# Perceiver attention kernel: where the second scores pause, and which step two projections stand in

## The chip, the cores and the metric

One core of a Trainium2 chip runs the whole program. The metric is the device time of one execution in microseconds (us); lower is better. The engines of the core run side by side and meet at semaphores: PE (TensorE, matmuls; PEld is its loading of weights), ACT (ScalarE, activations and evictions from the accumulator memory PSUM), DVE (VectorE, reductions and elementwise work), POOL (GpSimd, elementwise work) and SP, which issues the DMAs.

## The reference

There are 16 batches of 64 queries, a context of 1601 rows of width 256, and 16 heads of width 16. What matters here is the first part, cross attention whose temperature depends on statistics of its own scores:

```
K = ctx @ Wk.T + bk ; V = ctx @ Wv.T + bv ; Q = layernorm(x) @ Wq.T + bq
qk = Q . K                                  # per head, 64 x 1601
scores = qk / sqrt(16)
feats = [mean(scores), mean(max(scores)), mean(var(softmax(scores)))]
hidden = gelu(w1 feats + b1); hidden = gelu(w2 hidden + b2)
t = exp(clip(w3 hidden + b3, ln 0.1, ln 10))
out = softmax(qk / (2 t)) @ V ; x = x + out @ Wo.T + bo
```

After it come a gated recurrent layer and a feed-forward layer with quantised weights ("the tail"); they are computed for two batches at a time.

## The kernel before, in words

**Slots and steps.** The order of the work is written out by hand. A batch has a slot, and a slot has 32 steps; every engine walks through the same steps and takes from each its own part. In slot b the kernel computes the first scores of batch b, the statistics and the temperature of batch b-1, and the second scores (with the temperature) and the values of batch b-1 from step 14 on; those reach into steps 0 to 11 of the next slot. A tail piece of earlier batches lies in between. Below, a *full slot* is one in which all of this is there: slots 1 to 15 have first scores, statistics and projections (slot 1 has no second scores in its steps 0 to 11). Slot 0 has no statistics, slot 16 no first scores and no projections.

**First scores.** Unit u (step u) is one pair of heads, which takes 32 of the 128 rows of PE, against 400 keys (`scores`, L651); it shows as two matmul rows. DVE takes its maximum (`maxima`, L1179), ACT its exponential one step later (`exp1`, L909), DVE the sums of that two steps later (`sums`, L1185). There are three PSUM banks, so unit u on PE waits until ACT has done the exponential of unit u-3. PE issues units two at a time, in even steps. `S1_P` says which head pair a step takes, and so which row group (pair modulo 4).

**Second scores and values.** Unit v is one row group of one context tile of 256 rows (13 half tiles, 7 tiles, 4 row groups: 28 units). `S2_AT` is the list of the steps that units 0 to 27 stand in, with the steps of `S2_IDLE` left out: with (36, 37), which are steps 4 and 5 of the next slot, units 18 to 21 stand in steps 0 to 3, 22 and 23 in steps 6 and 7, 24 to 27 in steps 8 to 11. The row group of a unit is that of the first scores' pair two further, so that a first and a second score of one step take different row groups of PE. `scores2` (L667 adds a row, L677 the products) waits for the exponential of the unit two before, `exp2` (L918, ACT) comes one step later, `values` (L694) two steps after the scores and only where a unit stood two steps before; it waits for that unit's `exp2`.

**Projections.** `PJ_PLAN` gives the step in which PE projects the keys ("k", L605 or L612 by the form) or the values ("v") of a context tile: ("k", 4, 0) is the keys of tile 4 of the slot's own batch, a last number of 1 is the next batch's. In the profile the keys' matmuls are L605 (pjp<-cr,wkv) and the values' L612 (pjp<-wkv,cr), 12 to a projection. All projections use the one bank pjp: each waits (`pj_free`) until ACT has evicted the one before (L869 and L882), and ACT does that in the step after, behind `exp2` and `exp1` of that step. A projection of tile 5 must come behind the second scores (keys) or the values (values) that still read tile 5 of the batch before in the same buffer.

**Temperature.** `statistics` on DVE in steps 1, 3, 8 and 10. `temperature` on PE in steps 5, 6 and 7 (L631, L634, L636): in odd steps behind the step's projection, in step 6 between the second scores and the values. Between them ACT runs `gelu` (L888), at the end of step 5 and at the head of step 6, ahead of `exp2`, `exp1` and the eviction of step 6. Gelu and exp need different tables on ACT: there is an ACT_TABLE_LOAD ahead of the first gelu and one ahead of the next exponential.

**The context.** ACT splits a tile into a rounded part (`split_context`, L900), POOL makes the remainder one step later (L1083). Tile 5 is split in step 1, tile 6 in step 9. SP loads the raw tile for the next batch as soon as POOL is done with it.

Of the kernel before, what the change touches and what calls it, by code (L numbers as in the profile page):

```python
# [22 lines left out]
NPAIR = H // 2  # L23
# [35 lines left out]
def unit1(u):  # L59

    return u // NPAIR, S1_P[u]

# [1 line left out]

PJ_PLAN = [(1, ("k", 4, 0)), (5, ("v", 4, 0)), (7, ("k", 5, 0)), (9, ("v", 5, 0)), (11, ("k", 6, 0)),
           (12, ("v", 6, 0)), (13, ("m",)), (17, ("k", 0, 1)), (19, ("v", 0, 1)), (21, ("k", 1, 1)), (23, ("v", 1, 1)),
           (25, ("k", 2, 1)), (27, ("v", 2, 1)), (29, ("k", 3, 1)), (31, ("v", 3, 1))]
N_M = sum(w[0] == "m" for _, w in PJ_PLAN)  # L70
N_OLD = sum(w[0] != "m" and w[-1] == 0 for _, w in PJ_PLAN)
N_NEW = len(PJ_PLAN) - N_M - N_OLD

CTX_AT = {1: (5, 0), 9: (6, 0), 11: (0, 1), 15: (1, 1), 20: (2, 1), 24: (3, 1), 28: (4, 1)}
UNTIL = [(lo + w - 1) // (2 * P) for lo, w in CH]
S2_IDLE = (36, 37)
S2_AT = [s for s in range(14, 14 + S2U + 2) if s not in S2_IDLE]
S1_P = [0, 1, 2, 3, 6, 7, 4, 5, 2, 3, 0, 1, 4, 5, 6, 7] + 2 * list(range(NPAIR))
STATS_AT = [1, 3, 8, 10]
MLP_AT = {5: 0, 6: 1, 7: 2}  # L80
N_MLP = len(MLP_AT)
# [52 lines left out]
class Slot:  # L134
# [91 lines left out]
    def plan(self):  # L226

        got = []
        for step, what in PJ_PLAN:
            if what[0] == "m":  # L230
# [28 lines left out]
def build(nc, t, q_dram, out):  # L259
    ctx = ExitStack()  # L260
    with ctx:
# [298 lines left out]
        def _(pe):  # L560
# [93 lines left out]
            def unit2(v):  # L654

                k = 2 * (v // PPB)
                return k, (S1_P[S2_AT[v] % STEPS] + 2) % PPB, [min(P, SK - P * (k + i)) for i in range(min(2, KTILES - k))]

# [827 lines left out]
```

## Time and profile before

| what | us |
|---|---|
| median of 3 runs | 1311.03 (1310.67 to 1316.09) |
| the profiled execution's own time | 1311.66 |
| its span | 1309.4 |
| PE busy | 1155.3 (88%) |
| PE loading weights | 928.9 (71%) |
| DVE busy | 822.0 (63%) |
| ACT busy | 768.2 (59%) |
| POOL busy | 403.0 (31%) |

The span is the time between the first and the last event of the trace; the execution's own time is 2.3 us more. PE leads by far; no other engine is busy for two thirds of the span. The share of the DMA engines is small (10% of 16 engines). The mean granted clock of PE was 0.861 of full speed; it has two levels, 2.4 and 1.2 GHz (1.00 and 0.50 in the rows).

### The profile page before, as it was taken

The page shows a single profiled execution, that of the slowest core. Times are in us where ns is not written, and L with a number is a line of the kernel's source. Part 1 is how long each engine was busy: PE and PEld are TensorE (multiplying, and loading weights), DVE is VectorE, ACT ScalarE, POOL GpSimd, SP SyncE. Part 2 cuts the span into 40 slices and gives each one's busy share as a digit, 9 for nine tenths or more (in the row PEclk, how much of TensorE's full clock was granted, in tenths as well). Part 3 has the DMA queues.
Part 4 walks back from the last instruction along what each step waited for, and adds up shares of the span by engine and source line. Part 5 has one row for each costly group of instructions (what it writes and reads, how often), then busy time and mean ns, then how long its engine had stood idle before and what let it go on. Part 6 is the DMA issues. An engine that isn't in the chain of part 4 may idle for free.

```text
span 1309.4 us, 39200 instructions
## 1 busy us (share of the span) xinstructions
PE 1155.3 (88%) x14964; PEld 928.9 (71%) x14964; DVE 822.0 (63%) x2124; ACT 768.2 (59%) x1547; POOL 403.0 (31%) x416
## 2 busy tenths in 40 slices
PE   3767898989899989999899989998999989998935
PEld 3545687868787877878687878787777878776622
DVE  3458665656666766767666766676776766772232
ACT  2434486757666765667566766676566756672300
POOL 2366441313234313333233323431333323301210
PEclk9868697969888987989798988899898979995865
DMA  4500110101010101010110101010101000000000
GB/s 122 187 19 25 29 26 14 54 22 35 14 38 10 50 11 42 19 34 26 26 35 14 46 7 45 11 50 10 42 19 35 26 17 3 3 11 2 2 5 4
DMA packets 46812, 38.85 MB, mean 30 GB/s; under 512 B 14576, under 2 KB 46000, under 8 KB 46640
## 3 DMA queue, kind: packets, MB, share of 16 engines
q1 hardware_dynamic: 46640, 36.41, 10.2%
q8 instruction: 125, 2.05, 0.6%
q14 instruction: 47, 0.39, 0.1%
HBM read 34.30 MB, written 2.10 MB: 28 GB/s over the span
## 4 chain that ended last, share of the span: by engine, by line
PE 65%; DVE 16%; issue 9%; ACT 5%; POOL 2%; DMA 1%; SPq 1%; DVEq 0%; ACTq 0%; POOLq 0%
PE pjp L605 11%; PE pjp L612 11%; PE s2p L677 10%; PE s1p L651 10%; PE pvp L694 7%; DVE est L1185 4%; DVE negm L1179 3%; PE tlp L808 2%; PE tlp L790 2%; PE tlp L784 2%; PE s2p L667 1%; PE tlp L751 1%; PE tlp L771 1%; DVE feat L1202 1%; ACT ering L909 1%
## 5 line engine op out<-in xcount | busy, mean ns | idle before, releaser
L1179 DVE TENSOR_REDUCE negm<-s1p 128x1 f32<-128x400 f32 (+1 forms) x512 | 289.3, 565 | 227.1 <-PE s1p L651 222.5
L909 ACT ACTIVATE ering<-s1p,negm 128x400 f32<-128x400 f32 (+1 forms) x512 | 305.6, 597 | 142.7 <-DVE negm L1179 138.0
L918 ACT ACTIVATE pring<-s2p 128x512 f32<-128x512 f32 (+1 forms) x448 | 251.9, 567 | 152.4 <-PE s2p L677 151.9
L651 PE MATMUL s1p<-kt,qbd 32*128 32x400 f32 (+1 forms) x1024 | 301.0, 597 | 15.8 <-ACT ering L909 13.7
L1185 DVE BATCH_NORM_STATS2 est<-ering 128x6 f32<-128x400 f32 (+1 forms) x512 | 290.3, 567 | 23.4 <-ACT ering L909 23.4
L605 PE MATMUL pjp<-cr,wkv 128*128 128x256 f32 (+1 forms) x1344 | 219.4, 321 | 70.6 <-ACT vt L869 45.7
L605 PEld LDWEIGHTS pjp<-cr,wkv 128*128 128x128 f32 x1344 | 196.1, 223 | 87.8 <-issue 58.5
L677 PE MATMUL s2p<-q2bd,kt 32*128 32x128 f32 (+1 forms) x3328 | 249.7, 284 | 0.0
L677 PEld LDWEIGHTS s2p<-q2bd,kt 32*128 32x128 f32 (+1 forms) x3328 | 240.6, 195 | 7.5
L1083 POOL TENSOR_TENSOR cr<-stage,cr 128x512 fp32r<-128x512 f32 (+1 forms) x112 | 132.0, 1179 | 268.7 <-ACT cr L900 268.7
L612 PE MATMUL pjp<-wkv,cr 128*128 128x256 f32 (+1 forms) x1200 | 191.8, 314 | 11.7 <-ACT kt L882 11.4
L612 PEld LDWEIGHTS pjp<-wkv,cr 128*128 128x128 f32 (+1 forms) x1200 | 167.3, 208 | 30.2 <-ACT kt L882 17.7
L651 PEld LDWEIGHTS s1p<-kt,qbd 32*128 32x128 f32 x1024 | 99.1, 202 | 78.9 <-ACT ering L909 38.3
L1069 POOL TENSOR_TENSOR ksum<-ksum,kt 128x512 f32<-128x512 f32 (+1 forms) x80 | 82.6, 1033 | 225.8 <-ACT kt L882 225.7
L694 PE MATMUL pvp<-pring,vt 128*32 128x64 f32 x6656 | 151.2, 234 | 0.2
L694 PEld LDWEIGHTS pvp<-pring,vt 128*32 128x32 f32 x6656 | 112.3, 117 | 53.2 <-issue 24.4
L667 PE MATMUL s2p<-shrow,ones_r 32*128 32x512 f32 (+1 forms) x448 | 127.3, 503 | 5.9 <-ACT pring L918 4.6
L882 ACT ACTIVATE kt<-pjp 128x512 f32<-128x512 f32 (+1 forms) x112 | 61.7, 551 | 53.5 <-PE pjp L605 51.5
L1178 DVE COPY feat<-s1p 128x2 f32<-128x2 f32 x128 | 19.7, 154 | 87.8 <-PE s1p L651 87.2
L869 ACT ACTIVATE vt<-pjp 128x512 f32<-128x512 f32 (+1 forms) x108 | 61.0, 565 | 19.0 <-PE pjp L612 14.3
L900 ACT ACTIVATE cr<-stage 128x512 fp32r<-128x512 f32 (+1 forms) x112 | 65.3, 583 | 10.2 <-DMA stage<-in_ctx 10.2
L667 PEld LDWEIGHTS s2p<-shrow,ones_r 32*128 32x128 f32 (+1 forms) x448 | 48.0, 184 | 24.9 <-ACT pring L918 15.8
(186 smaller groups left out, 1008.8 us busy)
## 6 DMA issues: line engine op xcount, KB each, us to landing
stage<-in_ctx SPq DMA_DIRECT2D x96, 256.0 KB, 2.9
qbd<-q_dram SPq DMA_DIRECT2D x128, 8.0 KB, 1.7
stage<-in_ctx SPq DMA_DIRECT2D x16, 65.0 KB, 2.6
vt<-in_x SPq DMA_DIRECT2D x1, 1024.0 KB, 7.1
q_dram<-late SPq DMA_DIRECT2D x1, 1024.0 KB, 4.7
late<-in_x SPq DMA_DIRECT2D x8, 128.0 KB, 2.1
out_y<-late SPq DMA_DIRECT2D x8, 128.0 KB, 1.7
late<-in_gate SPq DMA_DIRECT2D x1, 768.0 KB, 5.0
```

The costliest lines, as they stand in the source:

```text
L605: mm = nc.tensor.matmul(bank[:, 2 * P * g:2 * P * g + n], wkv[:, 0, wp, d, P * g:P * g + P], c[:, cp, d, 0:n], start=(cp + wp + d == 0), s ...
L612: mm = nc.tensor.matmul(bank[0:m, D * j:D * j + D], c[:, cp, d, P * j:P * j + m], wkv[:, 1, wp, d, :], start=(cp + wp + d == 0), stop=((cp ...
L651: nc.tensor.matmul(s1p[u % 3][:, 0:w], qbd[s.par][rows, g, :], kt[s.par][rows, g, lo:lo + w], start=True, stop=True).then_inc(s1_full, 1)
L667: nc.tensor.matmul(s2p[v % 2][0:ms[0], 0:DB * P * n], ones_r[rows, 0:ms[0]], shrow[rows, :, :].unsqueeze(1).to_broadcast([RT, n, DB, P]), ...
L677: mm = nc.tensor.matmul(s2p[v % 2][0:ms[i], at:at + P], kt[1 - s.par][rows, g, lo:lo + ms[i]], q2bd[1 - s.par][rows, g, :], start=False, s ...
L694: mm = nc.tensor.matmul(pvp[32 * q:32 * q + 32, SQ * r:SQ * r + SQ], vhead(1 - s.par, k + i, ms[i], g, r, j), pring[0:ms[i], v % NPR, at:a ...
L909: nc.scalar.activation(ering[:, u % 3, 0:w], s1p[u % 3][:, 0:w], ACT.Exp, bias=negm[s.par][:, p, c:c + 1]).then_inc(s1_exp, 1)
L918: nc.scalar.activation(pring[0:m, v % NPR, 0:n], s2p[v % 2][0:m, 0:n], ACT.Exp).then_inc(s2_exp, 1)
L1069: nc.gpsimd.tensor_tensor(ksum[:, :, 0:m], was, k[:, :, 2 * P * w:2 * P * w + m], ALU.add).then_inc(ks_part, 1)
L1083: nc.gpsimd.tensor_tensor(c[:, 1, :, 0:n], stage[:, w, :, 0:n], c[:, 0, :, 0:n].bitcast(F32), ALU.subtract).then_inc(ctx_lo, 1)
L1179: nc.vector.tensor_reduce(negm[s.par][:, p, ch:ch + 1], s1p[u % 3][:, 0:w], AX.X, ALU.max, negate=True).then_inc(s1_max, 1)
L1185: nc.vector.bn_stats(est[:, p, ch, :], ering[:, u % 3, 0:CH[ch][1]]).then_inc(s1_sum, 1)
```

## The change

Three constants. The two steps without second scores become 38 and 39 (steps 6 and 7 of the next slot) in place of 36 and 37 (steps 4 and 5), so units 22 and 23 stand in steps 4 and 5. Their values follow two steps later, so `values` has nothing in step 8 in place of step 6. The values' projection of tile 4 goes from step 5 to step 3, the keys' projection of tile 5 from step 7 to step 5; step 7 has none. The order of the head pairs in steps 4 to 7 becomes 4, 5, 6, 7 in place of 6, 7, 4, 5, which keeps the four row groups of tile 5 complete.

```diff
-PJ_PLAN = [(1, ("k", 4, 0)), (5, ("v", 4, 0)), (7, ("k", 5, 0)), (9, ("v", 5, 0)), (11, ("k", 6, 0)),
+PJ_PLAN = [(1, ("k", 4, 0)), (3, ("v", 4, 0)), (5, ("k", 5, 0)), (9, ("v", 5, 0)), (11, ("k", 6, 0)),
            (12, ("v", 6, 0)), (13, ("m",)), (17, ("k", 0, 1)), (19, ("v", 0, 1)), (21, ("k", 1, 1)), (23, ("v", 1, 1)),
...
-S2_IDLE = (36, 37)
+S2_IDLE = (38, 39)
 S2_AT = [s for s in range(14, 14 + S2U + 2) if s not in S2_IDLE]
-S1_P = [0, 1, 2, 3, 6, 7, 4, 5, 2, 3, 0, 1, 4, 5, 6, 7] + 2 * list(range(NPAIR))
+S1_P = [0, 1, 2, 3, 4, 5, 6, 7, 2, 3, 0, 1, 4, 5, 6, 7] + 2 * list(range(NPAIR))
```

## Rows read from the trace of the kernel before

**Rows 1.** The waits from 100 us on: engine, line, releaser: us in total, times, longest.
```profile
PE pjp L605 <- ACT vt L869: 42.0, 15, 2.8
```
**Rows 2.** Timeline of PE, one slot, steps 2 to 12: start, us, then idle before.
```profile
616.89 0.60 PE L651 MATMUL s1p<-kt,qbd 32*128 32x400 f32 x2
...
618.23 0.65 PE L694 MATMUL pvp<-pring,vt 128*32 128x64 f32 x32
618.81 0.94 PE L651 MATMUL s1p<-kt,qbd 32*128 32x400 f32 x2
620.25 0.94 PE L651 MATMUL s1p<-kt,qbd 32*128 32x400 f32 x2 [0.50 <-ACT ering L909]
...
621.69 1.68 PE L612 MATMUL pjp<-wkv,cr 128*128 128x256 f32 x12
623.31 0.52 PE L631 MATMUL tlp<-fm,w1m 128*64 128x16 f32 x6
...
625.73 0.39 PE L634 MATMUL tlp<-hid,w2s 64*128 64x16 f32 x2 [0.18 <-ACT hid L888]
628.95 2.93 PE L605 MATMUL pjp<-cr,wkv 128*128 128x256 f32 x12 [2.83 <-ACT vt L869]
631.80 0.61 PE L636 MATMUL tlp<-hid,w3b 64*128 64x16 f32 x2
632.34 1.03 PE L651 MATMUL s1p<-kt,qbd 32*128 32x400 f32 x2
...
633.97 1.08 PE L694 MATMUL pvp<-pring,vt 128*32 128x64 f32 x32
634.98 2.80 PE L612 MATMUL pjp<-wkv,cr 128*128 128x256 f32 x12
637.71 0.60 PE L651 MATMUL s1p<-kt,qbd 32*128 32x400 f32 x2
...
641.04 0.94 PE L651 MATMUL s1p<-kt,qbd 32*128 32x400 f32 x4
```
**Rows 3.** Timeline of ACT in the same slot, steps 2 and 5 to 7.
```profile
616.71 0.60 ACT L882 ACTIVATE kt<-pjp 128x512 f32<-128x512 f32 x1
...
624.11 1.28 ACT L888 ACT_TABLE_LOAD   x1
...
626.44 1.28 ACT L909 ACT_TABLE_LOAD   x1
627.74 0.59 ACT L909 ACTIVATE ering<-s1p,negm 128x400 f32<-128x400 f32 x1
628.23 0.59 ACT L869 ACTIVATE vt<-pjp 128x512 f32<-128x512 f32 x1
```
**Rows 4.** The same slot on DVE and POOL: the statistics' last part; tile 5's remainder.
```profile
615.82 1.27 POOL L1083 TENSOR_TENSOR cr<-stage,cr 128x512 fp32r<-128x512 f32 x1 [6.31 <-ACT cr L900]
...
622.42 0.37 DVE L1225 TENSOR_SCALAR fm<-r,cst 128x8 f32<-128x8 f32 x2
```
**Rows 5.** Timeline of PE in the slot after it.
```profile
691.55 1.79 PE L651 MATMUL s1p<-kt,qbd 32*128 32x400 f32 x4
...
697.61 0.39 PE L634 MATMUL tlp<-hid,w2s 64*128 64x16 f32 x2 [0.19 <-ACT hid L888]
...
706.86 2.70 PE L612 MATMUL pjp<-wkv,cr 128*128 128x256 f32 x12
```
**Rows 6.** Windows: length, busy us of PE, PEld, DVE, ACT, POOL, then PE's clock, DMA.
```profile
605.60:609.00 3.40, 2.38 (x31) 2.15 (x32) 1.91 (x6) 1.89 (x5) 0.67 (x1) 1.00 0.28 77
...
647.70:651.10 3.40, 2.83 (x34) 1.67 (x36) 3.21 (x10) 2.61 (x6) 0.00 (x0) 1.00 0.44 119
651.10:654.60 3.50, 3.50 (x44) 3.15 (x36) 3.28 (x9) 1.18 (x3) 2.18 (x4) 0.51 0.00 0
...
627.30:637.50 10.20, 8.55 (x72) 7.44 (x72) 2.92 (x7) 6.00 (x14) 1.64 (x2) 0.50 0.01 2
...
132.40:152.90 20.50, 17.56 (x66) 13.31 (x68) 10.91 (x27) 8.09 (x19) 6.44 (x5) 0.50 0.08 20
```
**Rows 7.** Timeline of PE in slot 0: the values' projection of tile 5.
```profile
63.79 2.73 PE L612 MATMUL pjp<-wkv,cr 128*128 128x256 f32 x12 [3.66 <-ACT kt L882]
```

## The prediction

> **What bounds the kernel now.** I read the page's busy times first: PE is busy for 88% of the span and nothing else for two thirds, so what counts is where PE waits or runs slowly. The waits come next: from 100 us on, 15 keys' projections wait for ACT's eviction of the values' tile, 42.0 us together, 2.8 each [rows 1]. That is one wait in each of the full slots 1 to 15. The timeline of one slot shows its shape [rows 2]. PE finishes the second small matmul of the temperature at 625.73 + 0.39 = 626.12 and starts the keys' projection of tile 5 (step 7) at 628.95, after 2.83 idle. What it waits for is bank pjp, still holding the values of tile 4 (step 5, done at 623.31). ACT could evict them in step 6 only behind both gelus: a table load at 624.11, gelu, gelu, a load back at 626.44, one exponential at 627.74, the eviction at 628.23 to 628.82 [rows 3]. So ACT is closed to PE for 3.6 us (624.11 to 627.74), and the old order puts the one bank that PE needs behind it.
>
> The windows then show a second cost. PE's granted clock is 0.50 for the 10.2 us from 627.30 on [rows 6]. In it a values' projection takes 637.71 - 634.98 = 2.73 from start to start, against 623.31 - 621.69 = 1.62 at the high clock [rows 2]: 0.41 of dense time at the low clock is loss.
>
> Third, in step 4, where only two first scores stand, they follow each other: 618.81 and 620.25, with 0.50 idle for an exponential [rows 2]; in the next slot they take 1.79 [rows 5]. A pair that does not wait takes 0.94 (641.04, step 12) [rows 2]: the second unit waits there for `exp1` of unit 2, which is late behind the statistics on DVE.
>
> **The change part by part.** No instruction is added or removed; each has the work of before. So I lay PE's work out again from the end of step 2's values to the end of step 9's projection. Prices from start to start [rows 2]: a group of two first and two second scores 618.23 - 616.89 = 1.34; values 0.58; a projection 1.62; the temperature's first matmuls 0.52; a lone pair 0.94. At the low clock: the temperature's third 632.34 - 631.80 = 0.54, a group 1.63 (632.34 to 633.97).
>
> *Old:* from 618.81 to the start of step 9's projection at 634.98 is 16.17.
>
> *New, step 3:* the values of tile 4, 618.81 to 620.43. Its bank is free: ACT evicted tile 4's keys at 616.71 to 617.31 [rows 3]. This covers the late exponential of unit 2.
> *Step 4:* a whole group, to 621.77, and the values of units 20 and 21, to 622.35.
> *Step 5:* the keys of tile 5, to 623.97. Tile 4's values are evicted in ACT's step 4, in which it had idled; tile 5's remainder was made by POOL at 615.82 to 617.09 [rows 4]. Then the temperature's first, to 624.49; its inputs are ready at 622.79 [rows 4].
> *Step 6:* a lone pair, to 625.43. The table load at 624.11 stood in front of the gelu whether or not PE had come, and I take it to start there again, so the temperature's second is at 625.73 as before, to 626.12. ACT goes through gelu and load to 627.74, then `exp2` of unit 23, 0.59, to 628.33. PE has only the values of unit 22 (0.3) meanwhile, and waits to 628.45 for those of unit 23: some 2.0 us idle, which the change does not remove. It now stands in front of 0.5 us of values and no longer of a projection.
> *Steps 7 and 8:* at the low clock, values 0.5, the temperature's third 0.54, then a group of 1.63 in which first score 9 needs the exponential of unit 6. That comes behind `exp1` of unit 5 and the eviction of tile 5's keys. At ACT's spacing of 0.49 (627.74 to 628.23) [rows 3] it ends near 629.8, so I add 0.2. No values in step 8. Step 9's projection starts near 631.3, 3.7 earlier than 634.98.
>
> The next slot is like it, but PE there starts step 4 at 691.55, and 1.62 + 1.34 + 0.58 + 1.62 + 0.52 + 0.94 = 6.62 puts the temperature's second at 698.17, 0.56 later than the 697.61 of before. With the same 5.57 from there (631.3 - 625.73) the projection starts at 703.74, 3.1 before the old 706.86 [rows 5].
>
> **What the clock takes back.** If PE's low stretch begins and ends where it did, step 9's projection ends 3.7 earlier but 637.5 - 634.0 = 3.5 us of later work now falls into the low stretch, and loses 0.41 x 3.5 = 1.4. Net 3.7 - 1.4 = 2.3 in the one slot, 3.1 - 1.3 = 1.8 in the other, 2.05 as the mean, x 15 = 31. In other words: with the clock as it was, the gain is idle time and the lone pair, and not the slow projection.
>
> **Slots 0 and 16.** In slot 0 one projection more stands ahead of first scores 6 and 7, behind which DVE and POOL have their step's part of the weights' quantisation: at worst 2.7 later (the duration of a projection there); against it the wait of 3.66 for the eviction of the keys of tile 5, which now come two steps earlier, may go [rows 7]. I take 1 lost, between -3.7 and +2.7. Slot 16 I cost at nothing: it has no projections, and its second scores 22 and 23 still wait for the same exponentials.
>
> **Queues passed.** No DMA is moved. On SP tile 5's raw load waits for POOL in step 2, tile 6's in step 10, neither moved. POOL's key sum of tile 5 comes two steps earlier, in an idle stretch. ACT's evictions leave steps 6 and 8 for 4 and 6; the one in step 6 is again behind the gelus, but no projection waits for it until step 9. If that cover went, the old 2.8 would be back. What follows on PE from step 10 on waits only for work that comes earlier by the same amount.
>
> Sum: 1311.66 - 31 + 1 = 1281.7 for the profiled execution; it stood 0.6 above the median, so about 1281 as a median.
>
> **Rivals.**
> *A, the low clock gets shorter.* The idle piece is shorter (2.0 for 2.83) and less of what follows is slow. For it: a stretch of 3.4 with PE busy for 2.38 kept the full clock. Against it: another with 2.83 of 3.40 busy was followed by a low one [rows 6]. With 3.5 us less of low clock the 1.4 is not lost: 15 x 1.4 = 21 more, 1260. If it is gone altogether, the old losses go too (projections 2.93 - 1.68 and 2.80 - 1.68, values 1.08 - 0.65, a group 0.3: 3.1 a slot, x 15 = 47): 1281 - 47 = 1234.
> The Trainium skill, "TensorE: Matmul & The Clock Gate", section "HAM oscillation — how this bites in real kernels", says that a loop whose waits are long enough drops the clock in every iteration, and one with more work between them stays warm. By that rule alone the shortened wait might bring the 1234; the trace bears the first half out (low in each of these slots), and its drop after 2.83 of 3.40 busy speaks against the second.
> *B, the gain is smaller.* The wait at the gelus stays 2.8 instead of 2.0 (the first scores of step 8 also wait for ACT), and step 4's group is held by an exponential. About 1.1 less a slot: 31 - 16 = 15, so 1297.
> *C, the wait only moves.* If PE's chain is set by ACT through all of steps 5 to 9, PE gets nothing: 1311. Against it: the eviction and both exponentials behind the load are 0.49 apart, and PE's first wait is over at 628.45.
> *D, slower.* The low stretch gets longer, because what follows the wait is now thin (small matmuls, a pair that waits) where it was a dense projection. Slot 1, which has no second scores there, was low for 20.5 us [rows 6]. At 0.41 lost, ten more microseconds cost 4.2 a slot against 2.05 won: 15 x 2.15 = 32 slower, 1343. It decides from 5.0 us longer on (15.2 in place of 10.2). Against it: the step 9 projection and the group behind it are as dense as before.
> *E, the change isn't what it says* (the reordering kept PE in another order than the steps): not seen here, PE's rows follow the steps.
>
> **How the numbers follow.** Forecast 0.52 (1271 to 1291 by itself), A 0.24 (1234 to 1271), B 0.12, C 0.05, D 0.06, others 0.01. The time is that of the forecast. The range, 1243 to 1298, holds the forecast, B and all of A but its far end. About 0.5% is what a measurement can tell from no change; below 1304.5 are the forecast, A and B, 0.88; within it C and a part of B and D, 0.06; above it 0.06.
>
> **What would show it.** No wait of 2.8 for the values' eviction ahead of a keys' projection; the 42.0 of [rows 1] under 5. In its place 15 waits near 2.0 ahead of a values group, released by ACT's `exp2` (L918), right behind the second table load. Step 4 with a whole group and no 0.50; step 6 with a pair of 0.94. The keys of tile 5 at 1.6 to 1.7 instead of 2.9. The low stretch near 10 us a slot (A: near 7; D: 15 or more). A temperature's first matmul that comes earlier, or a wait above 2.8 there, would make it wrong.

## The result and the profile after

The changed kernel takes 1264.23 us as the median of 4 runs (1259.24 to 1266.11), against 1311.09 for the kernel before (4 runs, 1310.67 to 1316.09). The ratio is 0.9628, 95% interval 0.9591 to 0.9665: 47 us or 3.7% faster. The time lies in the stated range, but not where the forecast had put it (1281, own range 1271 to 1291); it lies where rival A stood (1260).

First the page of the changed kernel: busy time, share of the span, instructions.

```profile
span 1261.0 us, 39200 instructions
PE 1128.2 (89%) x14964; PEld 910.9 (72%) x14964; DVE 822.1 (65%) x2124; ACT 769.0 (61%) x1547; POOL 402.9 (32%) x416
```

The same 14964 matmuls take PE 27.1 us less busy time (1155.3 before), and the other engines as much as before. The span fell by 48.4, so 27.1 is shorter busy time and 21.3 is less idle time. Not all of the 27.1 is the clock, since busy time also holds what a pair waits inside. By the two levels and the mean granted clocks of the two executions (0.861 and 0.874), the time at the low level fell from 364 to 318 us; with the 0.41 of the prediction that is an estimate of 19 of the 27.1. The waits of PE for ACT in the changed kernel, over its whole run (us in total, times, longest):

```profile
PE pvp L694 <- ACT pring L918: 28.6, 15, 1.9
PE s1p L651 <- ACT ering L909: 10.1, 11, 2.5
...
PE pjp L605 <- ACT vt L869: 2.4, 3, 1.6
```

The 42.0 us of [rows 1] are gone from the keys' projection. In their place stand 15 waits of 1.9 ahead of values, released by the exponential (L918). One slot on PE, which answers to [rows 2]:

```profile
596.27 0.66 PE L694 MATMUL pvp<-pring,vt 128*32 128x64 f32 x32
596.85 1.68 PE L612 MATMUL pjp<-wkv,cr 128*128 128x256 f32 x12
598.46 0.60 PE L651 MATMUL s1p<-kt,qbd 32*128 32x400 f32 x2
...
600.67 1.68 PE L605 MATMUL pjp<-cr,wkv 128*128 128x256 f32 x12
602.28 0.52 PE L631 MATMUL tlp<-fm,w1m 128*64 128x16 f32 x6
602.74 0.94 PE L651 MATMUL s1p<-kt,qbd 32*128 32x400 f32 x4
603.77 0.39 PE L634 MATMUL tlp<-hid,w2s 64*128 64x16 f32 x2
604.09 0.43 PE L694 MATMUL pvp<-pring,vt 128*32 128x64 f32 x16
606.43 0.65 PE L694 MATMUL pvp<-pring,vt 128*32 128x64 f32 x16 [1.91 <-ACT pring L918]
607.01 0.61 PE L636 MATMUL tlp<-hid,w3b 64*128 64x16 f32 x2
...
609.51 2.80 PE L612 MATMUL pjp<-wkv,cr 128*128 128x256 f32 x12
612.24 0.60 PE L651 MATMUL s1p<-kt,qbd 32*128 32x400 f32 x2
```

From the end of step 2's values (596.85) to step 9's projection (609.51) it is 12.66, where it was 16.17. Both projections ahead of the wait now take 1.68, and the keys of tile 5 no longer 2.93; step 9's still takes 2.80, at the low clock. The lone pair takes 0.94. On ACT, the same moment, which answers to [rows 3]: the values' eviction now stands ahead of the loads, and behind them the exponential that PE waits for.

```profile
599.09 0.60 ACT L869 ACTIVATE vt<-pjp 128x512 f32<-128x512 f32 x1
...
602.15 1.28 ACT L888 ACT_TABLE_LOAD   x1
...
604.48 1.28 ACT L918 ACT_TABLE_LOAD   x1
605.78 0.60 ACT L918 ACTIVATE pring<-s2p 128x512 f32<-128x512 f32 x1
```

The low stretch of this slot and of the next, in windows (columns as in [rows 6]):

```profile
598.40:605.00 6.60, 6.03 (x96) 4.75 (x94) 5.63 (x18) 4.82 (x9) 0.00 (x0) 1.00 0.00 0
605.00:611.80 6.80, 5.37 (x42) 4.48 (x43) 3.16 (x8) 4.39 (x10) 1.18 (x1) 0.52 0.01 2
...
676.70:680.10 3.40, 3.40 (x22) 2.74 (x22) 2.37 (x6) 2.20 (x7) 1.24 (x2) 0.53 0.00 0
```

It is 6.8 us long in the one and 3.4 in the other, where it was 10.2 in both slots that the prediction used. The second of those, in the kernel before:

```profile
699.00:709.20 10.20, 8.37 (x71) 7.26 (x72) 3.14 (x8) 6.04 (x14) 4.34 (x4) 0.50 0.01 2
```

### The profile page after: what moved, and what is told of

Same layout as the page of the kernel before. It is cut to its first block, busy times and chain, and to the rows that moved or that the text cites. A ratio compares the mean times of both kernels' runs of the same rounds, so it can differ in the third digit from the quotient of the medians.

```text
span 1261.0 us, 39200 instructions
## 1 busy us (share of the span) xinstructions
PE 1128.2 (89%) x14964; PEld 910.9 (72%) x14964; DVE 822.1 (65%) x2124; ACT 769.0 (61%) x1547; POOL 402.9 (32%) x416
## 3 DMA queue, kind: packets, MB, share of 16 engines
q8 instruction: 125, 2.05, 0.7%
## 4 chain that ended last, share of the span: by engine, by line
PE 70%; DVE 12%; issue 8%; ACT 5%; POOL 2%; DMA 1%; SPq 1%; ACTq 0%; DVEq 0%; POOLq 0%
PE s1p L651 12%; PE s2p L677 12%; PE pjp L612 12%; PE pjp L605 11%; PE pvp L694 8%; DVE est L1185 2%; PE tlp L808 2%; DVE negm L1179 2%; PE tlp L790 2%; PE tlp L784 2%; PE s2p L667 2%; PE tlp L771 1%; ACT pring L918 1%; PE tlp L751 1%; PE tlp L729 1%
## 5 line engine op out<-in xcount | busy, mean ns | idle before, releaser
L918 ACT ACTIVATE pring<-s2p 128x512 f32<-128x512 f32 (+1 forms) x448 | 251.4, 565 | 158.5 <-PE s2p L677 158.0
L651 PE MATMUL s1p<-kt,qbd 32*128 32x400 f32 (+1 forms) x1024 | 292.3, 594 | 12.5 <-ACT ering L909 10.1
L605 PE MATMUL pjp<-cr,wkv 128*128 128x256 f32 (+1 forms) x1344 | 203.7, 306 | 26.5 <-DVE vt L1151 18.4
L605 PEld LDWEIGHTS pjp<-cr,wkv 128*128 128x128 f32 x1344 | 181.6, 208 | 44.8 <-issue 27.6
L694 PE MATMUL pvp<-pring,vt 128*32 128x64 f32 x6656 | 150.2, 230 | 28.7 <-ACT pring L918 28.6
L694 PEld LDWEIGHTS pvp<-pring,vt 128*32 128x32 f32 x6656 | 109.5, 114 | 68.1 <-ACT pring L918 32.4
```

The lines of the kernel that those rows point to most:

```text
L605: mm = nc.tensor.matmul(bank[:, 2 * P * g:2 * P * g + n], wkv[:, 0, wp, d, P * g:P * g + P], c[:, cp, d, 0:n], start=(cp + wp + d == 0), s ...
L651: nc.tensor.matmul(s1p[u % 3][:, 0:w], qbd[s.par][rows, g, :], kt[s.par][rows, g, lo:lo + w], start=True, stop=True).then_inc(s1_full, 1)
L694: mm = nc.tensor.matmul(pvp[32 * q:32 * q + 32, SQ * r:SQ * r + SQ], vhead(1 - s.par, k + i, ms[i], g, r, j), pring[0:ms[i], v % NPR, at:a ...
L918: nc.scalar.activation(pring[0:m, v % NPR, 0:n], s2p[v % 2][0:m, 0:n], ACT.Exp).then_inc(s2_exp, 1)
```

## The experiments

They were timed in three groups of four kernels, each against the kernel before on its own chip, so ratios are what compares (the kernel before had medians of 1313.6, 1314.9 and 1314.9 there). Brackets behind a ratio are its 95% interval. The letters T, P, K and so on are names for the expectations that stand ahead of each result.

**e1: only the values' projection of tile 4 moves.**

```diff
-PJ_PLAN = [(1, ("k", 4, 0)), (5, ("v", 4, 0)), (7, ("k", 5, 0)), ...
+PJ_PLAN = [(1, ("k", 4, 0)), (3, ("v", 4, 0)), (7, ("k", 5, 0)), ...
```


> The kernel before with one edit: the values' projection of tile 4 in step 3 in place of step 5; the pause of the second scores and the keys of tile 5 (step 7) stay. Theory T (what cost was bank pjp held by a tile whose eviction stands behind the gelus on ACT; the keys of tile 5 then have the bank free and run inside ACT's closed 3.6 us): the wait of 2.83 goes, the keys of tile 5 start right behind the temperature's second matmul and take 1.65, the first score of step 8 or 9 waits about 1 us for its exponential instead: 1265 to 1280. Rival P (the gain comes from the moved pause, which gives steps 4 and 5 full groups): 1305 to 1311, the wait only changes its name.

1271.24 us, ratio 0.9664 (0.9617 to 0.9711). T holds, P falls: one entry of the plan brings 42 us. In its trace the keys of tile 5 follow the temperature's second matmul at once (ends at 673.19 + 0.39, start 673.51), as forecast. The first score of step 8 shows a wait of 0.37, and more is hidden in the group's busy time: from there to the values it is 678.00 - 675.85 = 2.15, where a group takes 1.34. So the 1 us expected is there in all:

```profile
673.19 0.39 PE L634 MATMUL tlp<-hid,w2s 64*128 64x16 f32 x2 [0.19 <-ACT hid L888]
673.51 1.64 PE L605 MATMUL pjp<-cr,wkv 128*128 128x256 f32 x12
...
675.85 1.57 PE L651 MATMUL s1p<-kt,qbd 32*128 32x400 f32 x3 [0.37 <-ACT ering L909]
...
678.00 0.65 PE L694 MATMUL pvp<-pring,vt 128*32 128x64 f32 x32
678.59 2.93 PE L612 MATMUL pjp<-wkv,cr 128*128 128x256 f32 x12
```

What came back is mostly the length of the wait. In the profiled executions PE's idle time fell from 154.1 to 113.7 us and its busy time stayed (1155.3 and 1155.8); the mean clock went from 0.861 to 0.864, and in the middle of the run from 0.89 to 0.91 (columns as in [rows 6]). Step 9's projection still takes 2.93, with no long wait ahead of it.

```profile
200.00:1060.00 860.00, 835.11 (x11690) 690.80 (x11693) 608.98 (x1567) 594.31 (x1205) 278.03 (x301) 0.91 0.11 29
```

**e2: pause and values' projection, the keys of tile 5 left in step 7.**

```diff
-(3, ("v", 4, 0)), (5, ("k", 5, 0))
+(3, ("v", 4, 0)), (7, ("k", 5, 0))
```


> The changed kernel with the keys of tile 5 left in step 7: pause and values' projection moved. T: in steps 4 to 6 PE runs out of work early and waits some 1 us for the statistics and for exponential 4, then the wait of 1.9 for the values of unit 23, and only then the projection: about 1.5 to 2.5 us a slot worse than the changed kernel, 1285 to 1300. Rival K (where the keys of tile 5 stand is indifferent once the bank is free): 1260 to 1270.

1314.76 us, ratio 1.0003 (0.9981 to 1.0024): the whole gain is gone. K falls by 50 us; T had the direction and was 15 to 30 us short. Its slot has a pair that takes 1.63 in place of 0.94, then a wait of 0.65 and one of 1.91, with almost nothing between:

```profile
618.61 1.63 PE L651 MATMUL s1p<-kt,qbd 32*128 32x400 f32 x4
620.88 0.39 PE L634 MATMUL tlp<-hid,w2s 64*128 64x16 f32 x2 [0.65 <-ACT hid L888]
621.21 0.43 PE L694 MATMUL pvp<-pring,vt 128*32 128x64 f32 x16
623.55 0.65 PE L694 MATMUL pvp<-pring,vt 128*32 128x64 f32 x16 [1.91 <-ACT pring L918]
```

and over the middle of the run PE's clock is lower than even before. Windows from 200 to 1060 us, of the kernel before, of the changed one and of e2:

```profile
200.00:1060.00 860.00, 803.00 (x11237) 663.92 (x11230) 582.34 (x1505) 571.47 (x1157) 263.54 (x283) 0.89 0.11 28
```
```profile
200.00:1060.00 860.00, 820.44 (x11740) 681.39 (x11737) 611.18 (x1577) 595.85 (x1208) 278.65 (x302) 0.91 0.11 29
```
```profile
200.00:1060.00 860.00, 817.60 (x11182) 675.64 (x11175) 579.58 (x1497) 569.25 (x1148) 262.33 (x283) 0.88 0.11 28
```

e2 has PE as busy as the changed kernel (817.60 and 820.44 of 860) and gets 558 fewer matmuls done (11182 for 11740). Over the whole profiled executions it is the same: PE idles 136.7 us in e2 and 132.8 in the changed kernel, and is busy for 1172.1 and 1128.2, so 44 of the 48 us lie in busy time. By the mean clocks, 0.846 and 0.874, e2 has 85 us more at the low level, at 0.41 an estimate of 35 of the 44; fifteen pairs with 0.69 hidden in them would be another 10. T had counted the waits and not this.

**e3: only the pause moves.** The two edits of the pause and the pairs; `PJ_PLAN` as before.

> The kernel before with the pause moved to steps 6 and 7 alone (with the order of the pairs that it needs); both projections stay in steps 5 and 7. T: the eviction of tile 4's values is still behind the gelus, and now also behind exponential 23, so the keys of tile 5 start near 3.3 us after the temperature's second matmul as against 2.8 (0.9 of values lie in it): 1300 to 1315. Rival P: 1265 to 1280.

1325.91 us, ratio 1.0079 (1.0052 to 1.0106), slower by under 1% but clear of noise, and past the end of T's interval; P falls. The two waits follow each other, and the keys start 635.95 - 632.63 = 3.32 behind the temperature's second matmul (632.24 + 0.39), as T had it. What T left out is again busy time: PE is busy for 1190.2 us in place of 1155.3, and idle for less (140.2 in place of 154.1), at a mean clock of 0.838 in place of 0.861:

```profile
634.90 0.43 PE L694 MATMUL pvp<-pring,vt 128*32 128x64 f32 x16 [1.91 <-ACT pring L918]
635.95 2.26 PE L605 MATMUL pjp<-cr,wkv 128*128 128x256 f32 x12 [0.62 <-ACT vt L869]
```

The parts don't add: values' tile alone -42, pause alone +12, both +1, and with the keys of tile 5 in step 5 -47. The pause earns nothing by itself. It makes room for the keys' projection (which must stand behind the last second scores of tile 5), and only with that does it win back its cost. Between e1 and the full change there are some 5 us, and their intervals overlap.

**e4: the keys of tile 5 inside ACT's closed time.**

```diff
+                        if step == 6 and step in plan:
+                            project(s, *plan[step])      # behind temperature(s, 1), ahead of the values
-                    if step in plan:
+                    if step in plan and step != 6:
```


> The changed kernel with the keys of tile 5 not in step 5 but in step 6, between the temperature's second matmul and the values, so that 1.6 us of projection lie in ACT's closed time. T: the wait of 1.9 for exponential 23 shrinks to 0.3 or less, some 0.8 to 1.2 of idle time comes back in steps 5 and 6 (statistics, exponential 4) in the slots where PE is early, and PE's low clock stretch, 6.8 us a slot in the changed kernel, gets shorter or goes: 1235 to 1258. Rival Q (ACT's chain of load, exponentials 23, 5 and 6 sets the start of step 8 whatever PE does before): no gain, 1260 to 1266.

1262.53 us, ratio 0.9589 (0.9532 to 0.9647), not to be told from the changed kernel. The long wait is filled (PE's waits for L918 fell from 28.6 to 4.4 us), but a wait for the gelu came (10.1 us in 15), and in a slot where the statistics are waited for too (0.32 at 594.01) the keys of tile 5 still take 2.93, at the low clock. In the slot after it they take 1.69. T's interval is missed and Q's is met. But the mechanism of Q, that ACT sets the start of step 8 whatever PE does, is not what the trace has: step 8 starts 4.94 behind the temperature's second matmul in the first of these slots (601.65 - 596.71) and 3.34 in the second (669.52 - 666.18).

**e5 and e6: no table loads.** In both kernels:

```diff
-nc.scalar.activation(hid[:, n, :], tlp[0:DH, 0:H], ACT.Gelu,
+nc.scalar.activation(hid[:, n, :], tlp[0:DH, 0:H], ACT.Tanh,
```


> The kernel before with tanh in place of the two gelus of the temperature (another temperature, so another output): tanh is used elsewhere in this kernel without a table load beside exp, so both loads of 1.28 us should go. T (the wait is the two table loads with what is queued behind them): the wait ahead of the keys of tile 5 shrinks from 2.83 to about 0.3 to 0.8, the low clock behind it mostly goes, 1235 to 1260. Rival R (the wait is the round trip PE, ACT, PE itself and the order of ACT's work, the loads only fill it): above 1290.

> The changed kernel with tanh in place of the gelus. T: the change gains by moving work out from behind the table loads, so without loads it gains little: within 12 us of the tanh version of the kernel before, 1230 to 1250. Rival P2 (steps 4 and 6 are better filled whatever ACT does): 30 us or more below the tanh version of the kernel before.

1294.05 us, ratio 0.9833 (0.9805 to 0.9861), and 1243.21 us, ratio 0.9473 (0.9413 to 0.9533). My reading missed both times, and R and P2 hold (the time of e6 lies in my interval, but 51 us and not 12 below e5). Neither computes the reference. The loads are gone from the trace, and yet a wait of 1.40 is left in the kernel before, with a projection at the low clock behind it:

```profile
614.58 0.39 PE L634 MATMUL tlp<-hid,w2s 64*128 64x16 f32 x2
616.37 2.92 PE L605 MATMUL pjp<-cr,wkv 128*128 128x256 f32 x12 [1.40 <-ACT vt L869]
```
On ACT, the function in gelu's place, exponential and eviction follow one another there:

```profile
615.01 0.27 ACT L888 ACTIVATE hid<-tlp,cols 64x16 f32<-64x16 f32 x1 [1.66 <-PE tlp L634]
615.18 0.58 ACT L909 ACTIVATE ering<-s1p,negm 128x400 f32<-128x400 f32 x1
615.66 0.58 ACT L869 ACTIVATE vt<-pjp 128x512 f32<-128x512 f32 x1
```

Of 2.83, the loads make 1.43 and the round trip PE, ACT, PE with ACT's order the other 1.40. In e6 the wait that takes its place shrinks by the same 1.43, from 1.91 to 0.48:

```profile
592.98 0.43 PE L694 MATMUL pvp<-pring,vt 128*32 128x64 f32 x16 [0.48 <-ACT pring L918]
```

The change is worth 51 us without loads and 47 with them, so it does not live on the loads. What is left in e5 is the order on ACT: an eviction behind a function that itself waits for PE.

**e7 and e8: the wait filled with useless matmuls.** The kernel before with 18 and the changed one with 12:

```diff
+if step == 6 and s.has(1, B - 1):
+    for _ in range(12):
+        nc.tensor.matmul(pvp[:, 2 * P:4 * P], wkv[:, 0, 0, 0, 0:P], wkv[:, 1, 0, 0, :],
+                         start=s.b == 1, stop=True, skip_group_check=True)
```


> The kernel before with 18 idle-time matmuls added per slot of slots 1 to 15 (projection weights against projection weights, 128x256 each, 0.135 us at the high clock, 2.43 in all) between the temperature's second matmul and the keys of tile 5, into columns of the values' bank that nothing reads. They add work and take no wait away. T: the 10.2 us of low clock behind the wait come from PE's idleness; with the wait filled PE stays at the high clock and the kernel gets faster by up to 3.1 us a slot although it does more: 1265 to 1285. Rival S (the low clock has another cause, or comes anyway): 1311 to 1325, the filling itself at the low clock taking 4.9 us against a wait of 2.8.

> The changed kernel with 12 such matmuls (1.62 us at the high clock) between the values of unit 22 and those of unit 23, where PE waits 1.91 us. T: the 6.8 us of low clock that are left behind this wait go, 0.41 x 6.8 = 2.8 a slot or less: 1225 to 1250. Rival S: 1264 to 1290.

1273.93 us, ratio 0.969 (0.9661 to 0.9718), and 1243.81 us, ratio 0.9448 (0.9425 to 0.9471). S falls: added work makes the kernel before 41 us faster and the changed one some 24 us (0.9628 - 0.9448 of 1314.9; the intervals lie apart). In e7 the projection still waits for the same eviction and starts 2.84 behind the end of the same matmul (2.83 before), but it takes 1.67 in place of 2.93:

```profile
604.61 0.39 PE L634 MATMUL tlp<-hid,w2s 64*128 64x16 f32 x2 [0.19 <-ACT hid L893]
604.93 2.41 PE L833 MATMUL pvp<-wkv 128*128 128x256 f32 x18
607.84 1.67 PE L605 MATMUL pjp<-cr,wkv 128*128 128x256 f32 x12 [0.49 <-ACT vt L874]
```
In e8 a wait of 0.30 is left of 1.91, and step 9's projection takes 1.68 in place of 2.80:

```profile
594.52 0.43 PE L694 MATMUL pvp<-pring,vt 128*32 128x64 f32 x16 [0.30 <-ACT pring L923]
...
596.84 1.68 PE L612 MATMUL pjp<-wkv,cr 128*128 128x256 f32 x12
```
The clock's mean from 200 to 1060 us is 0.95 in e7, and in e8:

```profile
200.00:1060.00 860.00, 834.89 (x12213) 691.94 (x12212) 628.33 (x1622) 608.12 (x1236) 286.71 (x309) 0.97 0.11 29
```

**e9 to e12: where, and how much.** e9 puts the 12 behind the keys of tile 5 in step 5; e10 puts 6 in place of 12 into the wait; e11 is e4 with 4 ahead of the temperature's second matmul; e12 is e8 with 5 more in step 16, ahead of the values of unit 0.

```diff
 e9:  +if step == 5 and s.has(1, B - 1): 12 of them, behind project(s, *plan[step])
 e10: -for _ in range(12):   +for _ in range(6):
 e11: +if step == 6 and s.has(1, B - 1): 4 of them, ahead of temperature(s, MLP_AT[step])
 e12: +if s.has(1, B - 1): 5 of them, in values() for v == 0 behind the wait for fin_c
```


> Control for the filling matmuls: the changed kernel with the same 12 added per slot in step 5, right behind the keys of tile 5, where PE does not wait, in place of the wait. T2 (a filling matmul helps only by lying in a wait that would lower the clock): it costs its own time, 12 x 0.135 = 1.62 a slot, x 15 = 24, and leaves the wait of 1.9 and the low stretch: 1280 to 1292. Rival U (any added dense work near there keeps the clock high): 1240 to 1262.

1301.65 us, ratio 0.989 (0.986 to 0.992). U falls: in a dense place the same matmuls cost 34 us against the changed kernel (0.989 - 0.9628), more than their own 24. For the other 10 the trace has PE idle for 9.3 us more than in the changed kernel (142.1 and 132.8), 6.1 of it ahead of first scores that wait for an exponential (16.2 and 10.1 in all); why these came is open. The wait of 1.91 is left, as T2 said, but the time is past T2's interval.

> The changed kernel with 6 filling matmuls (0.81 us) in the wait of 1.9 in place of 12, so that about 1.1 us of it is left. T2: part of the low clock stays; between the changed kernel and the version with 12: 1246 to 1260. Rival V (a threshold: what matters is that some work lies there): 1240 to 1246.

1268.0 us, ratio 0.9658 (0.96 to 0.9715), no gain over the changed kernel (the intervals overlap). A wait of 1.01 is left, and the clock from 200 to 1060 us is 0.91 as without filling. So T2's "between" is wrong, and V too: half of the filling does not buy half of the clock.

```profile
602.37 0.97 PE L833 MATMUL pvp<-wkv 128*128 128x256 f32 x6
604.35 0.43 PE L694 MATMUL pvp<-pring,vt 128*32 128x64 f32 x16 [1.01 <-ACT pring L923]
```
```profile
200.00:1060.00 860.00, 834.73 (x11767) 690.52 (x11768) 610.25 (x1572) 596.38 (x1205) 277.74 (x301) 0.91 0.11 29
```

> The version with the keys of tile 5 in step 6, behind the temperature's second matmul, with 4 filling matmuls (0.54) in the wait of 0.65 that is left ahead of that second matmul. There real work fills the long wait. T2: the two low stretches that its trace still has in every second slot mostly go: 1238 to 1252. Rival Q (ACT's chain sets the start of step 8): no change, 1258 to 1266.

1272.34 us, ratio 0.9671 (0.9609 to 0.9732), a miss for T2 and for Q: the wait of 0.65 went, and the kernel is no faster than e4, by the medians 10 us slower (the ends of the two intervals overlap). The 60 added matmuls are 8 us of work. In the profiled executions PE idles 4.6 us less than in e4 and is busy for 19.0 more, at a mean clock of 0.869 for 0.876. Why the clock did not rise is open.

> The version with 12 filling matmuls in the changed kernel's wait (1243.8 measured) with 5 more (0.68) in step 16, ahead of the values of unit 0, where PE waits 0.82 for their exponential in slots 1 to 15. T2: some of the 3.4 us stretches of low clock behind that place go: 1232 to 1244. Rival W (a wait of 0.8 does not lower the clock and the filling delays nothing): 1244 to 1250.

1250.53 us, ratio 0.9522 (0.9467 to 0.9576), no better than e8, and above T2's interval; the clock's mean from 200 to 1060 us is 0.96 there. The wait of 0.82 that it was to fill is not in e8's trace: in the slot looked at, the values of unit 0 start at 547.37 with nothing idle ahead of them, and PE's waits ahead of values are 15 and 6.0 us in all, the number of those of unit 23. So e12 is one more case of work added where PE does not wait, and says nothing on a wait of 0.8.

e8 is the fastest of all kernels here that compute the reference, 1243.8 us.

## Why the prediction came out as it did

**What bounds (right).** The wait for the eviction of tile 4's values was what cost: e1, which takes only this away, brings 42 of 47 us, as much as the 42.0 of [rows 1].

**The layout of the steps (right).** Every piece stands where it was put: the values of unit 23 were given a wait of "some 2.0" and have 1.91, the temperature's second matmul to step 9's projection 5.57 and has 609.51 - 603.77 = 5.74, the lone pair 0.94, no wait in step 4. The projection of step 9 starts 16.17 - 12.66 = 3.51 earlier; the forecast had 3.7.

**The cause given for ACT's closed time (half right).** I put the 3.6 us down to the two loads and the gelus between them. e5 shows a wait of 1.40 without any load, and e6 a gain of the same size. For the sum this changed nothing.

**What the clock takes back (the step that failed).** The prediction said: "If PE's low stretch begins and ends where it did", and took 1.4 us a slot back. The stretch became 6.8 and 3.4 us where it had been 10.2. From the second temperature matmul of slot 1 to that of slot 15 the kernel before takes 1122.47 - 129.80 = 992.67 us and the changed one 1078.50 - 128.44 = 950.06: 42.6 in 14 slots, 3.04 a slot in place of 2.05. To step 9's projection the layout itself won 3.51 in the one slot and 3.33 in the other (706.86 - 691.55 = 15.31 before, 678.10 - 666.12 = 11.98 after), so the clock took back some 0.4 of that, by this estimate, and not 1.4. Rival A had priced this: 1.4 a slot, 21 in all, 1260. Its sign was there too: a low stretch "near 7" where the forecast had "near 10". I gave it 0.24, since the row with 2.83 of 3.40 busy had been followed by a low stretch [rows 6]. The time is in the stated range because that range took in most of A, and not because the forecast's own path was right.

The Trainium skill, "TensorE: Matmul & The Clock Gate", section "HAM oscillation — how this bites in real kernels", says that a loop with waits long against its work drops the clock in each round and one with enough work between them stays warm. e7 and e8 agree: with the wait filled the mean clock went to 0.95 and 0.97. With the wait shortened (the change) or gone (e1) it rose only from 0.89 to 0.91, so the rule gave the direction here and no size.

**Slot 0 (wrong sign, small).** I took 1 us lost. The pair behind the keys of tile 6 starts at 70.59 in place of 74.72, while the slot's first scores start 1.1 earlier (44.46 for 45.54): 3.0 won there. By slot 1 little is left of it: 129.80 - 128.44 = 1.4, of which 1.1 is the earlier start.

```profile
70.59 1.70 PE L651 MATMUL s1p<-kt,qbd 32*128 32x400 f32 x4
```

**The rest.** The wait of slot 15 lies behind the last of these matmuls. From there to the same matmul of slot 16 it is 54.90 before (1177.37) and 53.92 after (1132.42), so slot 15 won 1.0 where the sum had 2.05. The last 3.4 of the 48.4 lie behind that, in slot 16 and the tail, which were costed at nothing; no run shows what they are.

## What to carry to other kernels

An eviction that frees a bank should stand ahead of anything on its engine that waits for the matmul engine itself; moving one projection two steps forward did nearly all of this change. A pause in a pipeline costs or earns by what stands beside it: moved alone it lost 12 us, moved together with the right projections it lost nothing. Where PE waits in every round, look at the clock behind the wait too. The wait can cost twice, by its length and by the work behind it at half the clock, but the two need not come back together: e1 won mostly the length (42 us, the clock's mean in the middle of the run at 0.91), while e7 kept the length and won 41 us by the clock (0.95).

## What the hardware showed that I had not expected

- Matmuls whose output is never read made two kernels faster: 18 a slot by 41 us, 12 a slot by some 24 us, with PE's mean granted clock going from 0.89 to 0.95 and from 0.91 to 0.97.
- Half of them (6) in the same wait left clock and time as they were, and 12 in a place without a wait cost 34 us.
- Removing both table loads (2 x 1.28 us) shortened PE's wait by 1.43 in both kernels (2.83 to 1.40, and 1.91 to 0.48) and not by 2.56: the first load ran while PE had work of its own (624.11 to 625.39 in [rows 3]; PE idled 0.18 ahead of the matmul at 625.73).
- Taking the wait of 2.83 away with real work (e1) raised the mean clock from 0.89 to 0.91 only, where filling it with useless work (e7) raised it to 0.95.
